# A fused image-and-text kernel on one core: the edge convolution computed from split operands, with its halo rows staged on their own

## The chip, the cores and the metric

The kernel runs on one core of a Trainium2 chip. The metric is the device time of one execution in microseconds. The kernel before takes 2001.3 us, the median of three runs (1999.5 to 2003.4).

## What is computed

Eight images of 256 x 256 pixels and eight texts of 128 tokens go through one small transformer-like chain. The part that the change touches is the first step of each image:

```python
gray = jnp.einsum('bchw,c->bhw', x, w)[:, None]           # w = (0.2989, 0.587, 0.114)
edges = jax.lax.conv_general_dilated(gray, scharr, window_strides=(1, 1), padding='SAME', ...)
edge = jnp.sqrt(jnp.square(edges)).sum(axis=1) / 2        # two 3x3 filters, |.|, added
h = jnp.concatenate([edge, text_embedding], axis=1)       # 256 image rows + 128 text rows = 384 x 256
...                                                       # attention, MLP, ternary FFN, attention, mixture of 8 experts
```

So an image gives 256 rows of 256 numbers, from a gray picture and two 3x3 Scharr filters ("kinds" below: the horizontal and the vertical one). Everything after `h` works on 384 rows per image.

## The kernel before, in words

Every engine has its own program, written out by hand in one order, and engines wait for each other on semaphores. An engine executes in program order, so a wait holds back all that is written behind it on that engine.

**Stages.** A setup (weights, text embeddings, the filter matrices), a prologue for images 0 and 1, then sixteen "units": units 0 to 7 do the first attention and the MLPs, units 8 to 15 the second attention and more. The unit functions interleave three images: in unit u the attention of image u runs beside the MLP of image u-1 and the edge convolution of image u+2. Images 0 and 1 are convolved in setup and prologue, images 2 to 7 in units 0 to 5 (unit 0 is `U_FIRST`, units 1 to 5 are `U_MID0` in a loop). The last third of the time is routing and the expert stage.

**The convolution.** A picture is held as two halves of 128 rows, one row per partition: `gray[128, 2, 258]`, columns with a zero at either side. The sum over the three rows of a filter is a matrix product with a banded 128 x 128 matrix `band[:, k, dx, :]` (kind k, column shift dx). It is a product in full float32. For each half `hf` and kind `k` there are three such products of 256 columns, and a fourth with `edge_w` that brings in the one row of the other half (`halo_gray`, three shifted copies of it on three partitions):

```python
for k in range(2):
    o = ps[bank][:, IMG * k:IMG * (k + 1)]
    for dx in range(3):
        mm(o, band[:, k, dx, :], gray[:, hf, dx:dx + IMG], start=(dx == 0), stop=False)
    last = mm(o, edge_w[:, hf, k, :], halo_gray[:, 1 - hf, :], start=False, stop=True)
```

A PSUM bank (`conv0`, `conv1`) holds one half of the picture, both kinds. ScalarE takes the absolute value of a bank into `edge` (`edges` on ScalarE, line 1640), VectorE adds the two kinds into `h_in` (line 2128).

**Where it stands in a unit.** On VectorE `gray_ahead` (lines 2137 to 2141, three passes over the picture) stands early. SyncE then issues the six halo copies of one row each (`load_halo`, line 642), behind the load of the text rows and ahead of `load_residual` and of the load of the next image. On TensorE the order around it is: `turn(3)`, `attn_rows(2)`, `queries_keys(0)`, `edges(0)`, `scores(3)`, `edges(1)`, `queries_keys(1)`, `queries_keys(2)`, `mix(0)`. `queries_keys(0)` (line 1035, 128x512) needs the normalised, transposed input `xTa`, half of which ScalarE writes in `take_first` (line 1583) and half VectorE (line 2120). On ScalarE the order is `exps(0)`, `take_turned(0)`, `exps(1)`, `exps(2)`, `take_turned(1)`, `exps(3)`, `take_turned(2)`, `take_first`, `exps(4)`, `edge_sizes(0)`, `edge_sizes(1)`, `take_turned(3)`. The banks 6 and 7 of PSUM are handed from one dense product to the next: `conv0` is followed in its bank by `qk_1`, `conv1` by `qk_2`.

**Prologue.** TensorE multiplies `qk_0` to `qk_2` of image 0, then the convolution of image 1, then turns the stacked queries and keys; ScalarE takes the absolute values of image 1 and then writes `stk_q`, `stk_k` (line 1624).

Of the kernel before, what the change touches and what calls it, by code (L numbers as in the profile page):

```python
# [20 lines left out]
F32 = mybir.dt.float32  # L21
# [24 lines left out]
E = 8  # L46
# [22 lines left out]
for _name, _n in (("ident", P), ("rel", S), ("mask", S), ("cos", NT * 2 * HD0), ("sin", NT * 2 * HD0), ("ones", P),  # L69
                  ("shift", 3 * P), ("before", P), ("tiebreak", E * TILES), ("expert_row", E * TILES),  # L70
                  ("scan_keep", 2 * E * TILES), ("count", P), ("token", TILES), ("same_expert", GROUPS), ("bits", SEARCH * STEPS)):
    COLS[_name] = (NC_COLS, NC_COLS + _n)
    NC_COLS += _n
# [4 lines left out]
def shape_constants():  # L78

    c = np.zeros((P, NC_COLS), np.float32)  # L80

    def put(name, value):
        a, b = COLS[name]
        c[:, a:b] = np.asarray(value, np.float32).reshape(P, b - a)

    p = np.arange(P)
    put("ident", np.eye(P))
    rel = (S - P) + p[:, None] - np.arange(S)[None, :]
    put("rel", rel)
# [10 lines left out]
    put("shift", np.stack([np.eye(P, k=1 - dy) for dy in range(3)], 1))  # L100
    put("before", np.triu(np.ones((P, P)), 1))
# [222 lines left out]
FIRST_LOADS = 12  # L324
# [3 lines left out]
def early_fusion_kernel(nc, a, const, out):  # L328
# [23 lines left out]
    with ctx:  # L352
# [14 lines left out]
        def const_cols(name):  # L367
# [30 lines left out]
        (qk, rot2, stk_q, stk_k, img, gray, halo_gray), first_end = region(  # L398
            first_only, ("qk", [P, NT, 512], F32), ("rot2", [P, 512], F32),
            ("stk_q", [P, NT, 8 * 64], F32R), ("stk_k", [P, NT, 8 * 64], F32R),  # L400
            ("img", [P, 3, 2, IMG], F32), ("gray", [P, 2, IMG + 2], F32), ("halo_gray", [3, 2, IMG], F32))
# [5 lines left out]
        assert second_end <= first_end  # L407
        offsets["top"] = first_end
# [7 lines left out]
        band = sb("band", [P, 2, 3, P])  # L416
        edge_w = sb("edge_w", [3, 2, 2, P])
# [6 lines left out]
        edge = sb("edge", [P, 2, 2 * IMG])  # L424
# [25 lines left out]
        (wq1_rot, emb, embT, proj_raw, projT, txt_rows, hashf, hash_i, wq1_raw, rot_tmp, ang, scharr_b, scharr_h, shift_c,  # L450
# [5 lines left out]
            ("ang", [P, 8, H1], F32), ("scharr_b", [P, 2, 3, 3], F32), ("scharr_h", [3, 2, 3], F32),  # L456
            ("shift_c", [P, 3 * P], F32),
# [5 lines left out]
        txt_scale = small[:, 8:9]  # L463
        absum, above, below, gsum = small[:, 0:2], small[:, 2:4], small[:, 4:6], small[:, 6:8]
# [61 lines left out]
        gray_ready = sem("gray_ready")  # L526
        halo_loaded = sem("halo_loaded")
# [103 lines left out]
        def _(sp):  # L631
# [17 lines left out]
            for k, (dst, src) in enumerate((  # L649
# [9 lines left out]
                (scharr_h[:, 0, :], a["L0_tok_scharr"][0, 0].rearrange("a b -> b a")),  # L659
                (scharr_h[:, 1, :], a["L0_tok_scharr"][1, 0].rearrange("a b -> b a")),  # L660
                (shift_c[:], const[:, COLS["shift"][0]:COLS["shift"][1]]),
# [217 lines left out]
        def _(pe):  # L879
# [15 lines left out]
            def convolve(sec, i, img_no, halves):  # L895

                pe.wait_ge(gray_ready, at(img_no, 1, 1))
                pe.wait_ge(halo_loaded, at(img_no, 96, 96))
                for hf in halves:
                    name = f"conv{hf}"  # L900
                    bank = banks.bank(sec, name)
                    banks.wait_free(pe, sec, name, i)
                    for k in range(2):
                        o = ps[bank][:, IMG * k:IMG * (k + 1)]
                        for dx in range(3):
                            mm(o, band[:, k, dx, :], gray[:, hf, dx:dx + IMG], start=(dx == 0), stop=False)  # L906
                        last = mm(o, edge_w[:, hf, k, :], halo_gray[:, 1 - hf, :], start=False, stop=True)  # L907
                    last.then_inc(filled[bank], 1)
# [162 lines left out]
            def unit(sec, i, u, k):  # L1071
# [57 lines left out]
                def edges(hf):  # L1129
                    if k.conv:  # L1130
                        convolve(sec, i, moved(u, 2), (hf,))
# [440 lines left out]
        def _(act):  # L1572
# [61 lines left out]
            def edges(sec, i, img_no, hf):  # L1634


                banks.wait_filled(act, sec, f"conv{hf}", i)
                if img_no[0] is not None or img_no[1] > 0:
                    act.wait_ge(var_ready[LN_FIRST], at(img_no, NT, hf - NT + 1))
                f(edge[:, hf, :], ps[banks.bank(sec, f"conv{hf}")][:], ACT.Abs) \  # L1640
                    .then_inc(freed[banks.bank(sec, f"conv{hf}")], 1)
# [5 lines left out]
            def unit(sec, i, u, k):  # L1647
# [41 lines left out]
                def edge_sizes(hf):  # L1689
                    if k.conv:  # L1690
                        edges(sec, i, moved(u, 2), hf)
# [42 lines left out]
                if k.layer == 0:  # L1734
# [12 lines left out]
                    edge_sizes(0)  # L1747
                    edge_sizes(1)
# [126 lines left out]
            for hf in range(2):  # L1875
                edges(SETUP, 0, (None, 0), hf)
            ln_affine(PRO, 0, "lnA0", xTa[:, 0, :], 0, 2)
            for hf in range(2):
                edges(PRO, 0, (None, 1), hf)
# [70 lines left out]
        def _(dve):  # L1950
# [12 lines left out]
            v.memset(edge_w[:], 0.0)  # L1963
# [99 lines left out]
            shift = shift_c[:].rearrange("p (y m) -> p y m", y=3)  # L2063
            for y_ in range(3):
                for k in range(2):
                    for dx in range(3):
                        w = scharr_b[:, k, y_, dx:dx + 1]
                        if y_ == 0:
                            ts(band[:, k, dx, :], shift[:, 0, :], w, None, ALU.mult)
                        else:  # L2070
                            stt(band[:, k, dx, :], shift[:, y_, :], w, band[:, k, dx, :], ALU.mult, ALU.add)
                then()
            for k in range(2):
                ts(edge_w[:, 0, k, P - 1:P], scharr_h[:, k, 2:3], 0.5, None, ALU.mult)
                ts(edge_w[:, 1, k, 0:1], scharr_h[:, k, 0:1], 0.5, None, ALU.mult)
# [46 lines left out]
            def edges(sec, i, img_no, hf):  # L2122


                banks.wait_taken(dve, sec, f"conv{hf}", i)
                if img_no[0] is not None or img_no[1] > 0:
                    dve.wait_ge(spilled, at(img_no, 32, 0))
                tt(h_in[:, hf, :], edge[:, hf, 0:IMG], edge[:, hf, IMG:2 * IMG], ALU.add)

            def gray_image(c):  # L2130
# [3 lines left out]
                if c[0] is not None or c[1] > 0:  # L2134
                    dve.wait_ge(halo_loaded, at(c, 96, 0))
# [5 lines left out]
                stt(inner, img[:, 2], GRAY[2], inner, ALU.mult, ALU.add).then_inc(gray_ready, 1)  # L2141

# [112 lines left out]
            def unit(sec, i, u, k):  # L2255
# [54 lines left out]

                def edge_sum(hf):
                    if k.conv:
                        edges(sec, i, img_c, hf)
# [112 lines left out]
                if k.layer == 0:  # L2426
# [7 lines left out]
                    second_moments(0)  # L2434
                    take_values(1)
# [18 lines left out]
                    mask_max(6)  # L2454
                    edge_sum(0)
                    mlp_norm(1)
# [7 lines left out]
                    edge_sum(1)  # L2464
# [170 lines left out]
            for hf in range(2):  # L2635
                edges(SETUP, 0, (None, 0), hf)
# [6 lines left out]
            for hf in range(2):  # L2643
                edges(PRO, 0, (None, 1), hf)
# [281 lines left out]
        def _(pool):  # L2926
# [4 lines left out]
            g.memset(gray[:], 0.0)  # L2931
# [247 lines left out]
```

## Time and profile before

| | |
|---|---|
| median of three runs | 2001.3 us (1999.5 to 2003.4) |
| the profiled execution | 1996.8 us, its span 1995.0 us |
| TensorE matmul busy | 1768.5 us (89% of the span) |
| VectorE, ScalarE, GpSimd busy | 62%, 48%, 28% |
| mean granted TensorE clock | 0.943 of full |
| chain that ended last | TensorE 71%, issue 11%, VectorE 8% |

A time in a row is counted from the start of the span. In the timeline, the columns are start, duration, engine, line and operation, out<-in; a number in brackets is the idle time of that engine before it. "xN" are N instructions merged, the duration then being from the first start to the last end. A float32 product shows as two MATMUL records, a product from float32r operands as one. Matmul durations include the way through the array, so the pace of a sequence is read from the starts.

### The profile page before, as it was taken

The page shows a single profiled execution, that of the slowest core. Times are in us where ns is not written, and L with a number is a line of the kernel's source. Part 1 is how long each engine was busy: PE and PEld are TensorE (multiplying, and loading weights), DVE is VectorE, ACT ScalarE, POOL GpSimd, SP SyncE. Part 2 cuts the span into 40 slices and gives each one's busy share as a digit, 9 for nine tenths or more (in the row PEclk, how much of TensorE's full clock was granted, in tenths as well). Part 3 has the DMA queues.
Part 4 walks back from the last instruction along what each step waited for, and adds up shares of the span by engine and source line. Part 5 has one row for each costly group of instructions (what it writes and reads, how often), then busy time and mean ns, then how long its engine had stood idle before and what let it go on. Part 6 is the DMA issues. An engine that isn't in the chain of part 4 may idle for free.

```text
span 1995.0 us, 35526 instructions
## 1 busy us (share of the span) xinstructions
PE 1768.5 (89%) x10970; PEld 1408.1 (71%) x10970; DVE 1237.8 (62%) x4024; ACT 957.3 (48%) x2645; POOL 552.9 (28%) x784
## 2 busy tenths in 40 slices
PE   3457999999999899899999999992499999999997
PEld 2244676767677686667777777771389998999896
DVE  7446686767777676756677776657754454445442
ACT  2025474666657566565666666640033343333331
POOL 2233324242423411211111111001333335434431
PEclk9668999999999999999999999995589999999998
DMA  6100101101010100102100110002212222222210
GB/s 193 56 27 17 51 2 58 35 24 56 3 43 0 56 26 8 33 1 58 33 32 32 32 32 0 24 25 81 73 48 98 81 75 66 77 72 67 61 38 20
DMA packets 74577, 90.44 MB, mean 45 GB/s; under 512 B 16539, under 2 KB 64710, under 8 KB 74472
## 3 DMA queue, kind: packets, MB, share of 16 engines
q1 hardware_dynamic: 65000, 72.49, 11.1%
q0 software_dynamic: 9472, 16.77, 3.0%
q8 instruction: 39, 0.64, 0.1%
q14 instruction: 66, 0.54, 0.1%
HBM read 71.26 MB, written 25.26 MB: 48 GB/s over the span
## 4 chain that ended last, share of the span: by engine, by line
PE 71%; issue 11%; DVE 8%; POOL 3%; ACT 2%; DVEq 2%; DMA 1%; POOLq 1%; SPq 1%; ACTq 0%
PE bank L1035 17%; PE bank L1539 16%; PE bank L1554 9%; PE bank L983 6%; PE bank L967 5%; PE bank L1018 5%; PE bank L1177 2%; PE bank L906 2%; PE bank L994 1%; PE bank L1057 1%; DVE probs L2177 1%; PE bank L891 1%; DVE at_least L2735 1%; PE bank L907 1%; POOL rstd_a L2946 1%
## 5 line engine op out<-in xcount | busy, mean ns | idle before, releaser
L1660 ACT ACTIVATE probs<-probs,nmax 128x128 f32<-128x128 f32 (+2 forms) x768 | 381.0, 501 | 75.3 <-DVE nmax L2177 75.1
L983 PE MATMUL bank<-cst,probs 128*128 128x128 f32 x1536 | 234.5, 279 | 19.4 <-ACT probsT L1668 11.6
L983 PEld LDWEIGHTS bank<-cst,probs 128*128 128x128 f32 x1536 | 182.4, 143 | 68.4 <-issue 25.8
L1539 PE MATMUL bank<-xeT,gate_w 128*128 128x480 f32 x768 | 189.3, 382 | 1.4 <-issue 1.4
L1539 PE MATMUL bank<-xeT,up_w 128*128 128x480 f32 x768 | 188.2, 380 | 0.0
L2272 DVE COPY probsT<-bank 128x384 f32<-128x384 f32 x256 | 141.4, 552 | 74.0 <-PE bank L983 72.4
L1554 PE MATMUL bank<-down_w,hT 128*120 128x256 f32 x1536 | 182.8, 281 | 0.0
L1554 PEld LDWEIGHTS bank<-down_w,hT 128*120 128x120 f32 x1536 | 181.5, 182 | 0.1
L2988 POOL COPY rinv<-rowsum 128x384 f32<-128x384 f32 x80 | 40.7, 509 | 497.3 <-DVE o1T L2199 294.5
L2882 DVE TENSOR_TENSOR prod<-bank,sil 128x480 f32<-128x480 f32 x128 | 83.8, 657 | 150.5 <-PE bank L1539 150.3
L1668 ACT COPY probsT<-bank 128x384 f32<-128x384 f32 x256 | 121.8, 476 | 113.1 <-PE bank L983 104.4
L1539 PEld LDWEIGHTS bank<-xeT,gate_w 128*128 128x128 f32 x768 | 145.4, 190 | 23.2 <-issue 1.8
L1539 PEld LDWEIGHTS bank<-xeT,up_w 128*128 128x128 f32 x768 | 145.8, 190 | 21.9
L1583 ACT ACTIVATE sil<-bank 128x480 f32<-128x480 f32 x128 | 73.1, 571 | 181.5 <-PE bank L1539 181.5
L1660 ACT ACTIVATION_READ_ACCUMULATOR probs<-probs,nmax 128x1 f32 x768 | 147.0, 191 | 0.0
L3148 POOL DMA_INDIRECT out<-ye,slot_token x64 | 77.4, 1210 | 242.8 <-DVE ye L2896 230.9
L2177 DVE CUSTOM_DVE_ANT_0 probs<-bank,alibi 128x128 f32<-128x128 f32 (+2 forms) x384 | 141.2, 420 | 1.8
L2177 DVE CUSTOM_DVE_ANT_0 probs<-bank,cst 128x128 f32<-128x128 f32 (+2 forms) x384 | 140.4, 420 | 0.0
L967 PE MATMUL bank<-k1T,q1T 64*128 64x256 f32 (+2 forms) x768 | 100.5, 394 | 2.7 <-DVE nmax L2177 2.7
L3120 POOL DMA_INDIRECT xe<-xn_rows,slot_token x64 | 71.0, 1109 | 104.5 <-DVEq L2820 68.0
L967 PEld LDWEIGHTS bank<-k1T,q1T 64*128 64x128 f32 x768 | 83.3, 186 | 19.9 <-issue 15.2
L1018 PE MATMUL bank<-probsT,v 128*64 128x384 f32 (+2 forms) x768 | 97.0, 388 | 0.0
(314 smaller groups left out, 3325.1 us busy)
## 6 DMA issues: line engine op xcount, KB each, us to landing
gate_raw<-in_L_ffn_gate_w SPq DMA_DIRECT2D x8, 1024.0 KB, 4.8
up_raw<-in_L_ffn_up_w SPq DMA_DIRECT2D x8, 1024.0 KB, 6.9
down_raw<-in_L_ffn_down_w SPq DMA_DIRECT2D x8, 1024.0 KB, 5.7
img<-in_x SPq DMA_DIRECT2D x8, 768.0 KB, 5.1
residual_rows<-x SPq DMA_DIRECT2D x8, 384.0 KB, 2.5
residual_rows<-h_in SPq DMA_DIRECT2D x8, 384.0 KB, 3.8
xr<-residual_rows SPq DMA_DIRECT2D x8, 384.0 KB, 4.8
hr<-residual_rows SPq DMA_DIRECT2D x8, 384.0 KB, 3.7
```

The lines of the kernel that those rows point to most:

```text
L967: last = mm(scores_place(s, t), q[:, P * t:P * (t + 1)], k[:, 0:P * (t + 1)], start=True, stop=True)
L983: last = tr(ps[bank][:, P * q:P * (q + 1)], probs[:, n % 4, SEG[t] + P * j:SEG[t] + P * (j + 1)], ident)
L1018: last = mm(ps[5][rows_o, P * j:S], w, probsT[:, n % 4, cols_j], start=first, stop=final)
L1035: last = mm(ps[bank][:, 0:width], x, w, start=(k == 0), stop=(k == len(pieces) - 1))
L1539: last = mm(ps[bank][:, 0:HALF], w[:, wp, c, P * m:P * (m + 1)], xeT[:, xp, c, HALF * hf:HALF * (hf + 1)], start=(c == 0 and k == 0), stop ...
L1554: last = mm(ps[bank][:, D * (j % 2):D * (j % 2) + D][0:CP], hT[:, hp, m, CP * j:CP * (j + 1)], down_w[:, wp, m, :], start=(m == 0 and k == ...
L1660: last = f(p, p, ACT.Exp, bias=nmax[:, n % 4, t:t + 1], scale=-1.0, accum_out=rowsum[:, where, t:t + 1])
L1668: nc.scalar.copy(probsT[:, n % 4, 0:3 * P], ps[3][:, 0:3 * P]).then_inc(freed[3], 1)
L2177: last = v.tensor_tensor_reduce(out=probs[:, n % 4, seg(t)], in0=scores_place(n, t), in1=bias[:, P * (2 - t):S], scale=1.0, scalar=BIG, op ...
L2272: v.tensor_copy(probsT[:, n % 4, 3 * P:6 * P], ps[4][:, 0:3 * P]).then_inc(freed[4], 1)
L2882: tt(prod[:, q % 2, :], k[:, 0:HALF], sil[:, q % 2, :], ALU.mult).then_inc(f_, 1)
L3148: g.indirect_dma_start(out_rows, slots(e, j), ye[0:CP, j, :], None, bounds_check=T - 1, oob_is_err=False).then_inc(scattered, 16)
```

## The change

The picture and the filter matrices are split in an upper part in the short format float32r (`gray_hi`, `band[:, 0]`) and the remainder (`gray_lo`, `band[:, 1]`). Three products (hi x hi, hi x lo, lo x hi) take the place of one float32 product, each a single pass, and each over both halves of the picture at once, 512 columns. A bank now holds one kind, both halves. The halo rows of both halves and of all three parts are stacked on 18 partitions (`halo_rows`), spread by ScalarE into the two halves (`halo_halves`), and come in with one product per kind. The upper part of the picture is made on ScalarE (`gray_uppers`), the lower on VectorE (`gray_lowers`). The absolute value of the first kind is written to `h_in`, that of the second stays in its bank, and VectorE adds them from there; that bank is freed by VectorE.

```diff
             def load_halo(i):
-                sp.wait_ge(gray_ready, i + 1)
-                for k, row in enumerate((P - 1, 0)):
-                    for dx in range(3):
-                        sp.dma_start(halo_gray[dx:dx + 1, k, :], gray[row:row + 1, k, dx:dx + IMG]) \
-                            .then_inc(halo_loaded, 16)
+                sp.wait_ge(gray_split, i + 1)
+                if i > 0:
+                    sp.wait_ge(halo_ready, i)
+                for hf, row in enumerate((0, P - 1)):
+                    for part, src in enumerate((gray_hi, gray_lo, gray_hi)):
+                        for dx in range(3):
+                            q = 9 * hf + 3 * part + dx
+                            sp.dma_start(halo_rows[q:q + 1, :],
+                                         src[row:row + 1, 1 - hf, dx:dx + IMG].bitcast(F32)) \
+                                .then_inc(halo_loaded, 16)
...
-                pe.wait_ge(gray_ready, at(img_no, 1, 1))
-                pe.wait_ge(halo_loaded, at(img_no, 96, 96))
...
+                pe.wait_ge(gray_split, at(img_no, 1, 1))
+                pe.wait_ge(halo_ready, at(img_no, 1, 1))
+                for k in kinds:
...
+                    for dx in range(3):
+                        for w, x in ((0, gray_hi), (0, gray_lo), (1, gray_hi)):
+                            mm(ps[bank][:], band[:, w, k, dx, :], x[:, :, dx:dx + IMG],
+                               start=(dx == 0 and w == 0 and x is gray_hi), stop=False)
+                    mm(ps[bank][:], edge_w[:, k, :], halo[:], start=False, stop=True).then_inc(filled[bank], 1)
...
+            def halo_halves(img_no):
+                act.wait_ge(halo_loaded, at(img_no, 16 * HALO_LOADS, 16 * HALO_LOADS))
+                for hf in range(2):
+                    last = f(halo[:, hf, :], halo_rows[:], ACT.Identity, bias=0.0, scale=halo_side[:, hf:hf + 1])
+                last.then_inc(halo_ready, 1)
+
+            def gray_uppers(img_no):
+                act.wait_ge(gray_ready, at(img_no, 1, 1))
+                nc.scalar.copy(gray_hi[:, :, 1:IMG + 1], gray[:, :, 1:IMG + 1]).then_inc(gray_upper, 1)
...
                     exps(1)
+                    gray_upper_part()
                     exps(2)
                     take_turned(1)
                     exps(3)
                     take_turned(2)
+                    halo_parts()
                     take_second()
                     take_first()
                     exps(4)
                     take_queries(0)
-                    edge_sizes(0)
-                    edge_sizes(1)
+                    edge_sizes()
...
+            def gray_lowers(c):
+                dve.wait_ge(gray_upper, at(c, 1, 1))
+                inner = slice(1, IMG + 1)
+                tt(gray_lo[:, :, inner], gray[:, :, inner], gray_hi[:, :, inner].bitcast(F32), ALU.subtract).then_inc(gray_split, 1)
...
                     take_turned(0)
                     second_moments(0)
+                    gray_lower_part()
                     take_values(1)
...
                     mask_max(6)
+                    mlp_norm(1)
                     edge_sum(0)
-                    mlp_norm(1)
+                    edge_sum(1)
                     first_moments(0)
...
             for t in range(NT):
                 queries_keys_of(PRO, 0, t)
-            for hf in range(2):
-                edges(PRO, 0, (None, 1), hf)
+            gray_lowers((None, 1))
+            edges(PRO, 0, (None, 1))
```

In setup the filter matrices are split too (on VectorE: a copy and a subtraction of 768 columns and some ten tiny instructions, where four tiny ones stood), and there are four more small loads ahead of `first_loaded`. `gray` now lies where `gray_lo` lies.

## Rows read from the trace of the kernel before

**Rows 1.** The page's second part: busy tenths of TensorE and its granted clock, 40 slices.

```profile
PE   3457999999999899899999999992499999999997
...
PEclk9668999999999999999999999995589999999998
```

**Rows 2.** Busy time by stretch, one unit: length, busy us of each engine, clock, DMA.

```profile
483.40:571.90 88.50, 84.61 (x540) 63.38 (x540) 64.75 (x225) 54.94 (x160) 30.78 (x51) 1.00 0.11 33
```

**Rows 3.** Timeline of TensorE in unit 5, around the convolution of image 7.

```profile
585.33 1.88 PE L1035 MATMUL bank<-wqkv,xTa 128*128 128x512 f32 x4
587.05 1.46 PE L906 MATMUL bank<-gray,band 128*128 128x256 f32 x6
...
591.18 0.82 PE L967 MATMUL bank<-k0T,q0T 64*128 64x256 f32 x6
591.93 1.56 PE L906 MATMUL bank<-gray,band 128*128 128x256 f32 x6
...
596.16 3.70 PE L1035 MATMUL bank<-wqkv,xTa 128*128 128x512 f32 x8
```

**Rows 4.** Timeline of the expert stage on TensorE: six products of 480 columns, twice.

```profile
1474.62 1.46 PE L1539 MATMUL bank<-xeT,up_w 128*128 128x480 f32 x6
1475.92 1.46 PE L1539 MATMUL bank<-xeT,gate_w 128*128 128x480 f32 x6
```

**Rows 5.** Timelines of VectorE and ScalarE in unit 5, before the convolution.

```profile
578.16 0.69 DVE L2141 SCALAR_TENSOR_TENSOR gray<-img,gray 128x512 f32<-128x512 f32 x1
...
582.17 0.48 ACT L1668 COPY probsT<-bank 128x384 f32<-128x384 f32 x1 [0.35 <-PE bank L983]
583.64 0.67 ACT L1583 ACTIVATE xTa<-bank,cols 128x384 f32<-128x384 f32 x1 [0.99 <-PE bank L891]
```

**Rows 6.** The halo copies: timeline in unit 5, duration of all 48, time to landing.

```profile
578.88 3.66 SPq L642 DMA_DIRECT2D halo_gray<-gray  x6
...
L642 SPq DMA_DIRECT2D halo_gray<-gray x48: 497/589/1174, 59.1 to 582.0; - x48
...
DMA to landing us min/median/max: 1.6/1.7/2.4
```

**Rows 7.** Groups by form: busy us, mean ns of one, idle before.

```profile
L1581 ACT CAST f1T<-bank 128x512 fp32r<-128x512 f32 x4 | 2.3, 586 | 3.5 <-PE bank L942 3.5
...
L1624 ACT CAST stk_k<-qk 128x256 fp32r<-128x256 f32 x48 | 16.2, 403 | 0.0
...
L2887 DVE TENSOR_TENSOR hT<-prod,hT 128x480 fp32r<-128x480 f32 x128 | 83.2, 650 | 2.5 <-ACT hT L1929 2.0
...
L2377 DVE CAST hid_parts<-relu 128x384 fp32r<-128x384 f32 x32 | 11.4, 358 | 8.8 <-ACT relu L1583 8.7
```

**Rows 8.** Granted clock by stretch (length, TensorE busy, clock), and one timeline row.

```profile
71.00:72.00 1.00, 1.00 (x3) 0.60 0.00 0
...
146.00:147.00 1.00, 1.00 (x7) 0.56 0.32 86
...
141.56 1.19 PE L967 MATMUL bank<-k0T,q0T 64*128 64x256 f32 x6 [8.71 <-DVE nmax L2177]
```

**Rows 9.** Timeline of unit 0, image 2: end of the gray picture, first query-key product.

```profile
146.66 0.69 DVE L2141 SCALAR_TENSOR_TENSOR gray<-img,gray 128x512 f32<-128x512 f32 x1
...
151.91 1.94 PE L1035 MATMUL bank<-wqkv,xTa 128*128 128x512 f32 x4
```

**Rows 10.** Timeline of setup and prologue, images 0 and 1.

```profile
58.41 0.69 DVE L2141 SCALAR_TENSOR_TENSOR gray<-img,gray 128x512 f32<-128x512 f32 x1
...
64.30 2.90 PE L906 MATMUL bank<-gray,band 128*128 128x256 f32 x6 [15.19 <-DMA halo_gray<-gray]
...
76.41 0.60 ACT L1640 ACTIVATE edge<-bank 128x512 f32<-128x512 f32 x1 [3.56 <-PE bank L907]
...
99.00 0.69 DVE L2203 TENSOR_TENSOR qk<-bank,rows 128x512 f32<-128x512 f32 x1 [1.02 <-PE bank L1035]
...
111.02 1.01 ACT L1624 CAST stk_q<-qk 128x256 fp32r<-128x256 f32 x3 [3.16 <-POOL qk L2979]
```

More of the change, by code:

```diff
@@ L100, in shape_constants @@
     put("shift", np.stack([np.eye(P, k=1 - dy) for dy in range(3)], 1))
+    halo = np.zeros((P, 3))
+    for k in range(2):
+        halo[9 * k:9 * k + 9, k] = 1.0
+        halo[9 * k + 6:9 * k + 9, 2] = -1.0
+    put("halo", halo)
     put("before", np.triu(np.ones((P, P)), 1))
@@ L397, in early_fusion_kernel @@
         first_only = offsets["top"]
-        (qk, rot2, stk_q, stk_k, img, gray, halo_gray), first_end = region(
+        (qk, rot2, stk_q, stk_k, img, gray_hi, gray_lo, halo_rows, halo), first_end = region(
             first_only, ("qk", [P, NT, 512], F32), ("rot2", [P, 512], F32),
             ("stk_q", [P, NT, 8 * 64], F32R), ("stk_k", [P, NT, 8 * 64], F32R),
-            ("img", [P, 3, 2, IMG], F32), ("gray", [P, 2, IMG + 2], F32), ("halo_gray", [3, 2, IMG], F32))
+            ("img", [P, 3, 2, IMG], F32), ("gray_hi", [P, 2, IMG + 2], F32R), ("gray_lo", [P, 2, IMG + 2], F32R), ("halo_rows", [18, IMG], F32),
+            ("halo", [18, 2, IMG], F32R))
         (k1T, v1, _, q1T, x_moe, wq1, wk1, wv1), second_end = region(
@@ L407, in early_fusion_kernel @@
         assert second_end <= first_end
+        (gray,), _ = region(first_end - 4 * 3 * IMG - 32 * 65, ("gray", [P, 2, IMG + 2], F32))
         offsets["top"] = first_end
@@ L463, in early_fusion_kernel @@
         txt_scale = small[:, 8:9]
+        halo_side = small[0:18, 32:34]
         absum, above, below, gsum = small[:, 0:2], small[:, 2:4], small[:, 4:6], small[:, 6:8]
@@ L526, in early_fusion_kernel @@
         gray_ready = sem("gray_ready")
+        gray_upper = sem("gray_upper")
+        gray_split = sem("gray_split")
+        halo_ready = sem("halo_ready")
+        edge_ready = sem("edge_ready")
         halo_loaded = sem("halo_loaded")
@@ L893, in transposed, with convolve @@
                             last.then_inc(filled[bank], 1)
-            def convolve(sec, i, img_no, halves):
-                pe.wait_ge(gray_ready, at(img_no, 1, 1))
-                pe.wait_ge(halo_loaded, at(img_no, 96, 96))
-                for hf in halves:
-                    name = f"conv{hf}"
+            def convolve(sec, i, img_no, kinds):
+                pe.wait_ge(gray_split, at(img_no, 1, 1))
+                pe.wait_ge(halo_ready, at(img_no, 1, 1))
+                for k in kinds:
+                    name = f"conv{k}"
                     bank = banks.bank(sec, name)
                     banks.wait_free(pe, sec, name, i)
[L903 to L908, printed above, removed]
+                    for dx in range(3):
[3 more added lines that the diff above has]
+                    mm(ps[bank][:], edge_w[:, k, :], halo[:], start=False, stop=True).then_inc(filled[bank], 1)
             pe.wait_ge(first_loaded, 16 * FIRST_LOADS)
@@ L1127, in stack, with edges @@
                         stack_turned(sec, i, img_b, hh, t, x)
-                def edges(hf):
+                def edges(kind):
                     if k.conv:
-                        convolve(sec, i, moved(u, 2), (hf,))
+                        convolve(sec, i, moved(u, 2), (kind,))
                 def attn_rows(t):
@@ L1687, in take_stack, with gray_upper_part, halo_parts, edge_sizes @@
                         take_stack_of(sec, i, hh, t)
-                def edge_sizes(hf):
+                def gray_upper_part():
                     if k.conv:
-                        edges(sec, i, moved(u, 2), hf)
+                        gray_uppers(moved(u, 2))
+                def halo_parts():
+                    if k.conv:
+                        halo_halves(moved(u, 2))
+                def edge_sizes():
+                    if k.conv:
+                        edges(sec, i, moved(u, 2))
                 def take_mlp():
@@ L1873, in unit @@
                     relu_of(7)
-            for hf in range(2):
-                edges(SETUP, 0, (None, 0), hf)
+            gray_uppers((None, 0))
+            halo_halves((None, 0))
+            edges(SETUP, 0, (None, 0))
             ln_affine(PRO, 0, "lnA0", xTa[:, 0, :], 0, 2)
-            for hf in range(2):
-                edges(PRO, 0, (None, 1), hf)
+            gray_uppers((None, 1))
+            halo_halves((None, 1))
+            edges(PRO, 0, (None, 1))
             for hh in range(2):
@@ L1962, in _ @@
             v.memset(tok[:, :, 0:1], 0)
-            v.memset(edge_w[:], 0.0)
+            v.memset(small[:, 34:36], 0.0)
+            v.memset(edge_f[:], 0.0)
             v.memset(eps[:], EPS)
@@ L2120, in ln_affine, with edges @@
                     ts(dst, k[:, 0:S], cols[:, g:g + 1], cols[:, b:b + 1], ALU.mult, ALU.add).then_inc(f_, 1)
[L2122 to L2128, printed above, removed]
+            def edges(sec, i, img_no, halves=range(2)):
+                dve.wait_ge(edge_ready, at(img_no, 1, 1))
+                k, f_ = bank_of(sec, "conv1", i)
+                for hf in halves:
+                    last = tt(h_in[:, hf, :], h_in[:, hf, :], k[:, IMG * hf:IMG * (hf + 1)], ALU.add)
+                if 1 in halves:
+                    last.then_inc(f_, 1)
             def gray_image(c):
@@ L2309, in gray_ahead, with gray_lower_part @@
                         gray_image(img_c)
+                def gray_lower_part():
+                    if k.conv:
+                        gray_lowers(img_c)
                 def edge_sum(hf):
                     if k.conv:
-                        edges(sec, i, img_c, hf)
+                        edges(sec, i, img_c, (hf,))
                 def first_moments(t):
@@ L2634, in _ @@
             gray_image((None, 0))
-            for hf in range(2):
-                edges(SETUP, 0, (None, 0), hf)
+            gray_lowers((None, 0))
+            edges(SETUP, 0, (None, 0))
             embed((None, 0))
@@ L2642, in _ @@
                 queries_keys_of(PRO, 0, t)
-            for hf in range(2):
-                edges(PRO, 0, (None, 1), hf)
+            gray_lowers((None, 1))
+            edges(PRO, 0, (None, 1))
             for hh in range(2):
```

67 lines of the change are left out of this document (42 added, 25 removed).

## The prediction, made before the change was run

> **What bounds the kernel now.** I read the page's second part first. The reader sees TensorE at nine tenths or more from slice 5 to slice 26, which holds all units but the first two, at a granted clock of nine tenths or more; setup and prologue are the slices before, where TensorE is half idle and the clock is lower [rows 1]. Then the busy times of one unit: TensorE works 84.6 us of 88.5, and no other engine gets above 65 [rows 2]. So in units 0 to 5, where images 2 to 7 are convolved, TensorE sets the pace, and what its program waits for anywhere is added to the end. Last I read the timelines around the convolution, engine by engine, since the change puts new steps into the programs of all of them [rows 3, 5, 6].
>
> **What TensorE gains.** `edges(0)` runs from 587.05 to 591.18 and `edges(1)` from 591.93 to 596.16: 4.13 + 4.23 = 8.4 us per image [rows 3]. The new products are of the kind of the expert stage: six of 480 columns from one start to the next take 1.30 us, 0.217 each [rows 4], so 512 columns take 0.217 x 512/480 = 0.231 us. Two kinds of 9 + 1 products are 20 x 0.231 = 4.6 us. The gain is 3.7 us per image at full clock.
>
> **What now stands before the convolution.** The new chain, in unit 5: VectorE ends the gray picture at 578.16 + 0.69 = 578.85 [rows 5]. (1) `gray_uppers` on ScalarE, a cast of 512 columns, 0.59 [rows 7]; with the handover 0.65. It stands behind `exps(1)`, which is over by then. (2) `gray_lowers` on VectorE: 0.65 us for 480 columns [rows 7], so 0.7, with the handover 0.75. (3) SyncE may only now issue the copies, and there are 18 instead of 6. Six take 3.66 us from first start to last end, one takes 0.59 [rows 6]: the starts are (3.66 - 0.59)/5 = 0.61 apart. 17 such steps are 10.4 us; the first issue of a row is one of the short ones (497 ns the shortest), so the later steps are a little longer than the mean, and I take 10.7. (4) The last copy lands 1.7 us after its issue [rows 6]. (5) `halo_halves` on ScalarE, two instructions of 256 columns; the nearest is the cast of 256 columns, 0.40 each [rows 7]: 0.8. In all 0.65 + 0.75 + 0.05 + 10.7 + 1.7 + 0.8 = 14.65 us, so `halo_ready` comes at 593.5 in the old count of time.
>
> **Who waits for it.** The convolution itself would have been reached at 587.05. But `halo_halves` stands on ScalarE between `take_turned(2)`, which ends at 582.65, and `take_first`, which ran at 583.64 [rows 5]. So ScalarE stands still for about ten us, and behind it in its program are `take_first`, `exps(4)` and the absolute values. `take_first` (0.67) writes `xTa`, for which TensorE's `queries_keys(0)` waits, one step ahead of the convolution. That product starts at 593.5 + 0.7 = 594.2 instead of 585.33 [rows 3]: TensorE is held 8.9 us. VectorE runs dry too, because it waits for TensorE's products, so nobody has work in hand that could shorten the unit afterwards.
>
> **The clock after the hold.** TensorE has then been idle for some 8 us. In unit 0 it was idle 8.71 us before 141.56, and the clock, at half, is back at full only within the slice from 146 to 147, of which 0.56 on average means a change at 146.9 less a little, say 146.4 to 146.9 [rows 8]: five us at 1.2 instead of 2.4 GHz, 2.4 us lost. After the 15.19 us of idleness in setup it is back within the slice from 71 to 72, seven us after 64.30, 3.6 us lost [rows 8, 10]. The low bound is no loss at all. I take 2.4, the nearest row by length of idleness.
>
> **Per unit.** 8.9 + 2.4 - 3.7 = +7.6 us for images 3 to 7 (the distance from the gray picture to `queries_keys(0)`, 6.5 us in unit 5, repeats in the four other units of the loop within half a microsecond), 5 x 7.6 = 38. For image 2 the distance is 151.91 - 147.35 = 4.6 us instead of 6.5 [rows 9], so the hold is 10.8 and the sum +9.5. Units together: +47.5.
>
> **Setup, image 0.** VectorE's program is solid here. A cast of 768 columns is twice 0.36 and a subtraction of 768 about 1.0, from the forms of 384 and 480 columns [rows 7]; with some ten tiny instructions in place of four, 2.6 in all (2 to 3.5). From the end of the gray picture (59.10) TensorE started after 5.2 us [rows 10]; now after 14.65 + 0.4 for slightly slower issues here = 15.1: +9.9. The convolution took 64.3 to 76.4, mostly at half clock; 20 products, seven us of them at half clock (0.462 each), are 8.3 us: -3.8. Both sums on VectorE now follow the second absolute value, where one did: +0.4. The four extra small loads ahead of `first_loaded` would be 4 x 0.6 = 2.4 if all their issue counted; the big loads ahead of them fill the time, and I take 0.3. Together +9.4.
>
> **Prologue, image 1.** `gray_lowers` stands behind the third `queries_keys` of VectorE, which ends at 99.7 [rows 10]. From there 0.7 + 0.05 + 10.7 + 1.7 + 0.8: the convolution starts at 113.7, after 14 us without work, so again at half clock for most of its way, 7.1 to 8.3 us, and ends at 121 to 122. Two absolute values later, at 122.3, ScalarE begins `stk_q`, which ran at 111.02 [rows 10]: +11.3. Full clock would make it +8.
>
> **What I cost at nothing.** The bank of `conv1` is freed by VectorE after two sums, not by ScalarE: about 0.7 + 0.85 after the last product, while `qk_1` runs 1.7 us ahead of `qk_2`, its next user; without that cover it is a few tenths per unit. VectorE's wait for `gray_upper` and its subtraction delay `take_values(1)` by 0.9 us; the hold covers it, without a hold it would be 0.9 per unit. ScalarE is 0.6 us later in `exps(2)`; the same holds. `load_residual` and the next image sit on SyncE's queue behind 12 more copies, 7.5 us later; the first is wanted only with the MLP rows and so falls back less than TensorE, the second a unit later. The sum +47.5 + 9.4 + 11.3 = +68.2 is made on the profiled execution, 1996.8 us (span 1995.0 and 1.8 around it), and gives 2065; the median of the runs lies 4.5 us above that execution, so I predict **2069 us**.
>
> **A rule against this.** The profile shows SyncE occupied for 0.59 us by every one-row copy [rows 6]. The Trainium skill (DMA: Bandwidth & Descriptors, "Anatomy of one DMA", written for the gpsimd path) says that dispatch is small, about 50 ns, that many descriptors can be sent before it shows, and that nearly all of the fixed two microseconds is the wait for the write to be confirmed. By that rule 18 copies would land hardly later than one, and the hold would vanish; it is the first rival below. The row shows the time of the issue itself on this queue, and I go by the row.
>
> **Rivals.**
> (a) *The issues overlap and the chain hides.* Then `halo_ready` comes 0.65 + 0.75 + 1.7 + 0.8 + a little = 4 us after the picture, before the 6.5 us are over. Units: -3.7 + 0.9 each, six times, -17; setup 2.6 + 0.3 - 1 - 3.8 + 0.4 = -1.5; prologue nothing. Time 1983. For it speaks only that the data are 1 KB each; against it the six back-to-back issues. The point from which it decides is the sum of the issues: hold and gain cancel at 5.5 us for 17 steps, 0.32 us apart, half of what is seen. 4%.
> (b) *Held, but milder.* The clock does not fall, or recovers sooner (-2.4 x 6, -3 in the prologue), or issues come 0.50 apart, the shortest of 48 [rows 6] (17 x 0.13 x 8 = -18). One of them gives about 2050, both 2035. 20%.
> (c) *Held harder.* Some issues take up to 1.17 us [rows 6]; a mean of 0.73 adds 17 x 0.1 x 8 = 14; seven us of low clock add 1.2 x 6 = 7. Time 2076 to 2090. 17%.
> (d) *The products don't run at the pace of the expert stage.* At twice 0.231 us the convolution costs 9.2 us, +4.6 x 8 = +37, 2106. Against it speaks a row of the same form [rows 4]. 4%.
> (e) *A partly hidden hold, to within 0.2%* (4 us, about what can be told from no change): 2%.
> My forecast, within 10 us of 2069, has 53%.
>
> **Range.** From (b)'s double case to above (c): 2037 to 2092, with a little over 8 in 10. Faster by over 0.2%: (a), 4%; within 0.2%: (e), 2%; slower: 94%.
>
> **What would show it.** In a unit: 18 halo issues over 11 us; ScalarE idle about ten us before two 18x256 instructions; TensorE idle eight us before `queries_keys(0)` and the clock at half for the next five; the convolution itself 4.6 us where the clock is full; idle time ahead of the first expert unchanged. Most likely to make me wrong: another pace of 18 issues, which counts eight times.

## The result, and the profile after

| | kernel before | changed kernel |
|---|---|---|
| median of the runs | 2002.3 us (1999.5 to 2005.1) | 2095.3 us (2093.5 to 2099.6) |
| profiled execution, its span | 1996.8 us, 1995.0 us | 2095.4 us, 2093.6 us |
| mean clock granted to TensorE | 0.943 | 0.918 |

The ratio is 1.0467, 95% interval 1.0445 to 1.0490: the change made the kernel 4.7% slower. The forecast was slower, 2069 us with 2037 to 2092 as the range; the sign is right, the median lies 3 us above the range. From profile to profile the loss is 98.6 us, where the sum said 68.2.

The page's second part after the change, 40 slices, stands beside [rows 1]:

```profile
PE   3255779879797999989999999996269999999997
...
PEclk9557699999999999999999999998569999999998
```

The stretch of low clock at the start is one slice longer and a step lower, and in the units up to slice 13 TensorE shows more digits of seven and eight. Busy time of one unit (columns as in [rows 2]):

```profile
455.20:553.80 98.60, 85.92 (x534) 64.17 (x532) 65.47 (x227) 56.51 (x163) 30.59 (x51) 0.93 0.10 30
```

A unit takes 98.6 us instead of 88.5, and TensorE is busy in it for 1.3 us more only, at a mean clock of 0.93. So about nine us are idleness. Where they lie, the timelines of unit 5 show. First TensorE, from the last work before the hold (the stretch in which TensorE waits) to the end of the convolution; in brackets the idle time before, and what ended it:

```profile
656.85 1.13 PE L1053 MATMUL bank<-wo,o0T 128*128 128x256 f32 x4 [0.61 <-DVE vpad L2296]
...
660.39 0.76 PE L910 MATMUL bank<-cst,xh_a 128*128 128x128 f32 x5 [0.79 <-DVE vpad L2296]
661.00 0.82 PE L1001 MATMUL bank<-cst,probs 128*128 128x128 f32 x6
670.41 2.08 PE L1053 MATMUL bank<-wo,o0T 128*128 128x256 f32 x4 [8.59 <-ACT xTa L1601]
672.27 3.62 PE L1053 MATMUL bank<-wqkv,xTa 128*128 128x512 f32 x4
674.91 1.42 PE L924 MATMUL bank<-gray_hi,band 128*128 128x512 f32 x1
...
679.40 0.50 PE L924 MATMUL bank<-gray_hi,band 128*128 128x512 f32 x1
...
681.71 0.50 PE L926 MATMUL bank<-halo,edge_w 18*128 18x512 f32 x1
682.13 3.70 PE L1053 MATMUL bank<-wqkv,xTa 128*128 128x512 f32 x8
```

ScalarE and SyncE in the same stretch:

```profile
655.05 0.62 ACT L1660 CAST gray_hi<-gray 128x512 fp32r<-128x512 f32 x1 [0.39 <-DVE gray L2200]
...
668.89 0.91 ACT L1655 ACTIVATE halo<-halo_rows,small 18x256 fp32r<-18x256 f32 x2 [9.20 <-DMA halo_rows<-gray_hi]
669.71 0.65 ACT L1601 ACTIVATE xTa<-bank,cols 128x384 f32<-128x384 f32 x1
```

```profile
656.42 1.77 SPq L660 DMA_DIRECT2D halo_rows<-gray_hi  x3
...
665.87 1.85 SPq L660 DMA_DIRECT2D halo_rows<-gray_hi  x3
```

The reader sees the chain as it was forecast: picture, cast, subtraction, 18 issues from 656.42 to 667.72, landing, and two instructions of ScalarE that stood 9.20 us before a wait, with `take_first` behind them. But the first product behind the hold is not `queries_keys(0)`: it is one of `wo` and `o0T`, `attn_rows(2)`.

Second, a stretch with which the change has nothing to do. Waits in layer 1 (VectorE runs its units 9 to 14 as a loop) and the route to the experts: of TensorE, then of VectorE; the numbers are us in all, times, longest:

```profile
PE bank L985 <- DVE nmax L2241: 5.5, 5, 1.3
PE bank L1012 <- POOL rinv L3056: 4.6, 5, 1.0
```

```profile
DVE rowsum L2255 <- issue: 9.6, 5, 2.0
...
DVE probs L2241 <- issue: 2.7, 5, 0.7
```

None of these four stands there in the kernel before, although the instructions of that loop are the same, in the same order. "Issue" is time in which an engine waited for nothing that the profile shows. The page counts 92 packets on the instruction queue instead of 66, and 25 of them fall between 1067 and 1340 us, where there were 2 in the same stretch (980 to 1253) before.

### The profile page after: what moved, and what is told of

Read it like the earlier page. It is cut to its first block, busy times and chain, and to the rows that moved or that the text cites. A ratio compares the mean times of both kernels' runs of the same rounds, so it can differ in the third digit from the quotient of the medians.

```text
span 2093.6 us, 35492 instructions
## 1 busy us (share of the span) xinstructions
PE 1773.8 (85%) x10874; PEld 1408.4 (67%) x10874; DVE 1245.2 (59%) x4040; ACT 969.5 (46%) x2669; POOL 551.5 (26%) x783
## 3 DMA queue, kind: packets, MB, share of 16 engines
q1 hardware_dynamic: 68102, 72.59, 10.8%
## 4 chain that ended last, share of the span: by engine, by line
PE 61%; issue 12%; DVE 8%; POOL 6%; SPq 4%; POOLq 2%; ACT 2%; DMA 2%; DVEq 1%; ACTq 0%
PE bank L1557 16%; PE bank L1053 14%; PE bank L1572 9%; PE bank L1001 5%; PE bank L1036 5%; PE bank L985 5%; SPq L660 3%; PE bank L1195 2%; POOL rot L3039 1%; PE bank L1075 1%; DVE probs L2241 1%; PE bank L1012 1%; DVE at_least L2804 1%; POOL qk L3047 1%; POOL rstd_a L3014 1%
## 5 line engine op out<-in xcount | busy, mean ns | idle before, releaser
L1053 PE MATMUL bank<-wqkv,xTa 128*128 128x512 f32 (+1 forms) x192 | 87.8, 596 | 15.9 <-ACT xTa L1601 10.4
```

What stands on the lines that cost most here:

```text
L1053: last = mm(ps[bank][:, 0:width], x, w, start=(k == 0), stop=(k == len(pieces) - 1))
```

## The experiments

Each ratio is to the kernel before.

**Two first tries on the layer-1 loop.** The edit, ahead of VectorE's loop over units 9 to 14, with 13 in the kernel before and 64 in the changed one:

```diff
+            for _ in range(13):
+                v.nop()
             with dve.Fori(0, MID1) as i:
```

> The kernel before with 13 empty instructions put into VectorE's program just ahead of its loop of layer-1 units (13 is by how much the change lengthened that program). Theory (code loading): the loop of units 9 to 14 no longer stays loaded, VectorE stands still 2.0 us at each of 5 jumps back, TensorE waits about 1 us for rinv and 1 us for nmax after each; +10 to +12 us, about 2013. Rival: the loss in layer 1 comes from the changed memory places or from the late start of layer 1, not from the length of the program; then 13 empty instructions cost nothing, 2002.

> The changed kernel with 64 empty instructions at the same place, so that the loop lies in other blocks of the program again. Theory (code loading): the waits for rinv and nmax in units 9 to 14 go, -10 to -12, the 64 instructions cost at most 3 once: 2084 to 2088. Rival (memory places or lateness): 2095 or a little above.

Measured: 1998.8 us, 0.9993 (0.9977 to 1.0010), and 2095.0 us, 1.0469 (1.0442 to 1.0497). Nothing follows from this about the loop: the empty instructions are not in the built programs (the second profile counts 35492 instructions, as that of the changed kernel does), so both runs repeat the old programs, and show how well the times hold. The same two experiments with one-element memsets, which are kept, 17 in the kernel before and 64 in the changed one:

```diff
+            for j in range(17):
+                v.memset(small[32 * (j // 32):32 * (j // 32) + 1, 36 + j % 32:37 + j % 32], 0.0)
             with dve.Fori(0, MID1) as i:
```

> The kernel before with 17 one-element memsets of an unused place in VectorE's program just ahead of its loop of layer-1 units; with them the loop lies exactly where it lies in the changed kernel (the changed kernel's program for VectorE is 17 instructions longer up to there; the empty instructions of the first try were dropped when the program was built, so that it was the kernel before). Theory (code loading by the place of the loop): VectorE stands still some 2 us at each of 5 jumps back, TensorE waits for rinv and nmax after each, +10 to +12: 2012 to 2014. Rival (memory places or lateness): 1 us for the memsets at most, 2001 to 2003.

> The changed kernel with 64 such memsets at the same place (a first try with empty instructions left the program as it was), so that the loop begins at the start of a block of 256 instructions. Theory (code loading): the stands of VectorE and the waits of TensorE for rinv and nmax in units 9 to 14 go, -10 to -12, the memsets cost 1 to 3 once: 2084 to 2087. Rival: 2095 to 2098.

Measured: 2011.3 us, 1.0053 (1.0035 to 1.0071), which is 10.3 us more than before; and 2083.5 us, 1.0405 (1.0384 to 1.0425), 11.7 us less than the changed kernel. Waits of VectorE and TensorE in the kernel before with 17 memsets, over the layer-1 stretch:

```profile
DVE rowsum L2191 <- issue: 9.7, 5, 2.0
```

```profile
PE bank L967 <- DVE nmax L2177: 7.1, 6, 1.5
PE bank L994 <- POOL rinv L2990: 4.7, 5, 1.0
```

The waits appear with the 17 memsets and go with the 64. The instruction queue has 91 packets instead of 66 in the first, 68 instead of 92 in the second. So 10 to 12 us of the loss come from where the loop of layer 1 lies in VectorE's program, which by my count the change made 17 instructions longer ahead of it (13 by the first count). The Trainium skill (Runtime: NRT & Kernel Launch, "Instruction fetch mechanics") says that instructions are fetched in blocks of 256, that two blocks are held, and that a jump to a block not held must wait for it. The trace agrees as to the kind of wait: five stands of some 2 us, 62 us apart, one for each jump back of a loop of six. Which places of the loop are free of the waits the runs do not show, beyond the three tried: the old one, 17 instructions on, and 64 beyond that.

Waits of the same look stand in the kernel before as well, in the loop of units 1 to 5, one for each of its four jumps back. VectorE and, behind it, TensorE:

```profile
DVE rowsum L2193 <- issue: 12.3, 4, 3.3
```

```profile
PE bank L994 <- POOL rinv L2988: 11.5, 4, 3.1
```

They are in every version here, and no run tried to remove them. That another place of this loop would free up to 11 us is an estimate from these rows, not shown. They matter below, because the clock sometimes falls behind them.

**The wait on ScalarE moved behind `take_queries(0)`.**

```diff
                     take_turned(2)
-                    halo_parts()
                     take_second()
                     take_first()
                     exps(4)
                     take_queries(0)
+                    halo_parts()
                     edge_sizes()
```

> The changed kernel, but ScalarE's wait for the halo rows and its two copies stand directly ahead of the absolute values, behind take_first, exps(4) and take_queries(0). Theory (the hold is one of program order on ScalarE): the chain from the gray picture to halo_ready stays at 14.7 us, but TensorE now does attn_rows(2) and queries_keys(0), about 3 to 4 us of work, before it stops at the convolution; -3.5 in each of five units, -2 in unit 0: about 2075 (2071 to 2080). Rival 1: the clock falls as long, and VectorE or ScalarE run dry anyway, so nothing is gained: 2095. Rival 2: the hold is not set by this chain at all: 2095.

Measured: 2080.4 us, 1.0396 (1.0372 to 1.0421), 15 us less than the changed kernel. TensorE in unit 5:

```profile
648.29 1.88 PE L1053 MATMUL bank<-wqkv,xTa 128*128 128x512 f32 x4
655.68 0.79 PE L924 MATMUL bank<-gray_hi,band 128*128 128x512 f32 x1 [5.52 <-ACT halo L1655]
```

The products that were held are now done first, and the idle time is 5.5 instead of 8.6 us. From unit 2 on the gray pictures follow one another at 95.2 to 95.6 us instead of 98.5 to 98.9: there the order on ScalarE is worth 3.3 us a unit, close to the 3.5 expected. In unit 1 it is worth 0.7 only, because the clock stayed at half for longer behind the hold. The chain is there still.

**Six copies of three rows.**

```diff
-                        for dx in range(3):
-                            q = 9 * hf + 3 * part + dx
-                            sp.dma_start(halo_rows[q:q + 1, :],
-                                         src[row:row + 1, 1 - hf, dx:dx + IMG].bitcast(F32)) \
-                                .then_inc(halo_loaded, 16)
+                        q = 9 * hf + 3 * part
+                        rows = src[row:row + 1, 1 - hf, 0:IMG].bitcast(F32)
+                        rows = bass.AP(rows.tensor, rows.offset, [list(rows.ap[0]), [1, 3], [1, IMG]])
+                        sp.dma_start(halo_rows[q:q + 3, :], rows).then_inc(halo_loaded, 16)
```

> The changed kernel, but with 6 halo copies of three shifted rows each instead of 18 of one row; the same bytes, the order on ScalarE as in the changed kernel. Theory (SyncE pays 0.6 us per copy, whatever it holds): 12 copies less make the chain 7.5 us shorter, 7.2 instead of 14.7 us; the hold in a unit falls from 9.9 to 2.4 and the clock does not fall, so a unit takes 88.6 + 2.4 - 2.9 = 88.1; setup loses 2 instead of 9.4, the prologue 5.6 to 7 instead of 14; with the 12 us of layer 1 that stay, about 2016 (2012 to 2024). Rival: the time goes by row, a copy of three rows takes 1.8 us; then all stays as it is, 2095.

Measured: 2030.0 us, 1.0143 (1.0116 to 1.0170): 65 us of the 93 are gone. The halo copies (ns shortest/median/longest), then TensorE in unit 5:

```profile
L661 SPq DMA_DIRECT2D halo_rows<-gray_hi x32: 630/631/842, 64.2 to 601.5; - x32
```

```profile
604.76 2.08 PE L1052 MATMUL bank<-wo,o0T 128*128 128x256 f32 x4 [1.28 <-ACT xTa L1600]
606.63 2.66 PE L1052 MATMUL bank<-wqkv,xTa 128*128 128x512 f32 x4
```

A copy of three rows occupies SyncE for 0.63 us, one of a single row for 0.59 [rows 6]: the price is by the copy. The hold is 1.28 us. But the time is 14 us above what I expected. In this unit `attn_rows(2)` takes 2.08 us where its like takes 1.13 at full clock: the granted clock is 0.50 from 605 to 608 and 0.91 in the next microsecond. The four units before it do not show that. Their holds were 0.72 to 1.30 us, and behind each of them the same four products ran at full clock. In three of these units the clock had fallen earlier, behind TensorE's stand for `rinv`. Unit 4 has both:

```profile
502.28 0.85 PE L1011 MATMUL bank<-cst,rinv 128*128 128x128 f32 x3 [2.77 <-POOL rinv L3055]
502.92 1.91 PE L1052 MATMUL bank<-wqkv,xTa 128*128 128x256 f32 x4
...
515.48 1.13 PE L1052 MATMUL bank<-wo,o0T 128*128 128x256 f32 x4 [1.28 <-ACT xTa L1600]
```

So neither stand brings the clock down by itself each time. Added up over slices of a microsecond (TensorE's busy time times the missing share of the clock), 10.7 us are lost to it between 230 and 700 us, against 1.5 in the same stretch of the kernel before (215 to 680). These 9 us are the largest piece of what the expectation lacked; the waits for `vpad` (0.6 to 0.8 us, once or twice a unit) and unit 0 (4.7 us longer than before) are others. Why the clock falls behind one such stand and not behind the next stays open.

**Both together.**

> Six copies of three rows and ScalarE's wait directly ahead of the absolute values, both together; VectorE's program as in the changed kernel. Theory: halo_ready comes 7.3 us after the gray picture, TensorE reaches the convolution 8.2 us or more after it, so nothing is held; what stays of the cost in a unit are the two waits for vpad behind gray_lowers, 1.4 us, against a convolution 2.9 us shorter: a unit takes 87.1, 2.5 to 3 less than with six copies alone, 2012 to 2016 in all. Rival: the 1.4 us of waits are enough to bring the clock down for 4 us, 2 us a unit: 2024 to 2028.

Measured: 2046.2 us, 1.0230 (1.0209 to 1.0251), 16 us more than with six copies alone. Both theories missed. ScalarE in unit 5:

```profile
614.94 0.67 ACT L1600 ACTIVATE xTa<-bank,cols 128x384 f32<-128x384 f32 x1 [1.40 <-PE bank L909]
619.27 0.40 ACT L1690 ACTIVATE probs<-probs,nmax 128x128 f32<-128x128 f32 x1 [3.67 <-DVE nmax L2240]
...
620.76 0.89 ACT L1654 ACTIVATE halo<-halo_rows,small 18x256 fp32r<-18x256 f32 x2
```

`halo_parts` has no wait of its own any more, but it stands behind `exps(4)`, which waits for a maximum of VectorE. TensorE stood 3.38 us before the convolution, and then the clock was low from 621.9 to 631. In units 1 to 4 the same stand of 3.37 to 3.40 us was followed by about three us at half clock in three cases and by none at all in the fourth (530 us). One microsecond each (length, TensorE busy, TensorE weight load, VectorE, ScalarE, GpSimd, clock, DMA share, GB/s):

```profile
622.00:623.00 1.00, 1.00 (x3) 0.81 (x4) 0.00 (x0) 0.00 (x0) 1.00 (x2) 0.50 0.00 0
...
630.00:631.00 1.00, 1.00 (x3) 0.75 (x3) 0.00 (x0) 0.00 (x0) 0.00 (x0) 0.51 0.00 0
631.00:632.00 1.00, 1.00 (x4) 0.37 (x2) 0.00 (x0) 0.00 (x0) 0.00 (x0) 1.00 0.00 0
```

**The same with the other losses taken away.** The last kernel, with `gray_lowers` behind the first `queries_keys` of the prologue and behind `take_values(1)` in a unit, and with the 64 memsets:

```diff
             for t in range(NT):
                 queries_keys_of(PRO, 0, t)
-            gray_lowers((None, 1))
+                if t == 0:
+                    gray_lowers((None, 1))
...
-                    gray_lower_part()
                     take_values(1)
+                    gray_lower_part()
```

> As the last, and besides: gray_lowers behind take_values(1) in a unit, in the prologue gray_lowers behind the first of the three queries_keys of VectorE, and 64 memsets ahead of the layer-1 loop. Theory: no wait for vpad (-1.4 x 6), no code loading in layer 1 (-10), the prologue's convolution is no longer behind the queries_keys (-4 to -8): 1983 to 1995, that is 0.3 to 0.9% faster than the kernel before. Rival (the clock or another wait takes the place of those removed): 2005 or more.

Measured: 2035.5 us, 1.0158 (1.0135 to 1.0180). The prologue and layer 1 gave what they were to give (`stk_q` began at 112.95 instead of 120.07, and the layer-1 waits are gone), but the hold of 3.38 us was the same, and the last units took 95.5 us: the clock now stayed at half for nine us behind it in four units, and over units 1 to 5 it took back nine us of what was gained (26.8 lost, counted as above, against 18.0). Four edits at once told less here than the next three did.

**The two instructions between `take_first` and `exps(4)`.** Six copies, and:

```diff
-                    halo_parts()
                     take_second()
                     take_first()
+                    halo_parts()
                     exps(4)
```

> Six copies of three rows, and ScalarE's two halo instructions directly behind take_first, ahead of exps(4). Theory: behind exps(4) they stood behind the maxima of VectorE (ScalarE waited 3.67 us for nmax and came to them 12 us after the gray picture, the rows having landed at 6.5); ahead of exps(4) they run 7.5 us after the picture, 1.5 to 2 us before TensorE reaches the convolution. No hold, clock at full: a unit 88.6 - 2.9 + 1.4 (the waits for vpad behind gray_lowers) = 87.1; 2012 to 2017. Rival: the 1.4 us of waits bring the clock down by themselves; 2022 to 2030.

> As the last, with the 64 memsets ahead of the layer-1 loop and gray_lowers behind the first queries_keys of the prologue. Theory: -11 (code) and -7 (prologue, as in the run before): 1994 to 1999, faster than the kernel before by 0.1 to 0.4%. Rival with the clock: 2004 to 2012.

> As the last, and in a unit gray_lowers behind take_values(1). Theory: one of the two waits for vpad (0.6) goes, the halo comes 0.9 us later and stays just hidden: -0.6 x 6 against the last, 1990 to 1996. Rival: halo_halves now comes later than TensorE, a short hold, and with it the clock: above the last by 5 or more.

Measured: the first, 2017.9 us, 1.0088 (1.0070 to 1.0105); the second, with memsets and prologue, 1998.4 us, 0.9988 (0.9977 to 0.9999); the third, with `gray_lowers` behind `take_values(1)` too, 2001.2 us, 1.0003 (0.9992 to 1.0014). The second is the best version. Its gain of 0.12% is too small to count (its executions lie between 1995 and 2001 us, those of the kernel before between 1996 and 2005), but it is the changed convolution at no loss. The third has no hold either; it lost 7.7 us to the clock over these units where the second lost 4.6, which is about its distance from it. TensorE and ScalarE in unit 5 of the second:

```profile
583.70 0.77 PE L909 MATMUL bank<-cst,xh_a 128*128 128x128 f32 x5 [0.78 <-DVE vpad L2295]
...
586.08 1.88 PE L1052 MATMUL bank<-wqkv,xTa 128*128 128x512 f32 x4
587.40 0.80 PE L923 MATMUL bank<-gray_hi,band 128*128 128x512 f32 x1
```

```profile
584.39 0.67 ACT L1600 ACTIVATE xTa<-bank,cols 128x384 f32<-128x384 f32 x1 [1.40 <-PE bank L909]
584.96 0.89 ACT L1654 ACTIVATE halo<-halo_rows,small 18x256 fp32r<-18x256 f32 x2
```

`halo_ready` comes at 585.85, 1.5 us before TensorE wants it, and no wait for `halo` is left in a unit. Even so a unit takes 88.0 to 89.0 us (88.5 to 89.7 before), not the 87.1 that I expected: 0.8 to 1.4 us go to the waits for `vpad` behind `gray_lowers` (0.2 to 0.4 before), and in unit 5 the clock is 0.77 from 570 to 575 and 0.88 from 575 to 580, behind the same stand for `rinv` (2.79 us) that left it at 1.00 in the kernel before (2.81 us). Nearly all of the gain of the products is used up.

## Why the prediction was right in kind and too low in size

**The chain: right.** Forecast 14.65 us from the end of the gray picture to `halo_ready`; in unit 5 it is 655.02 to 669.80, 14.8. That it costs by the number of copies is shown by the six-copy run, and the first rival, by which the issues overlap and the time would be 1983, has fallen. The Trainium skill (DMA: Bandwidth & Descriptors, "Anatomy of one DMA") gives some 50 ns for the dispatch of a DMA on the gpsimd path. That figure can't be carried over to SyncE's queue: here each copy occupies the engine for 0.59 to 0.63 us. The point from which I said that rival decides, 5.5 us of issues, held only with the place on ScalarE mended: at 4.0 us of issues a unit still lost 0.5 to 1.7 us in the one place, and in the other it lay between 1.1 us gained and 0.4 lost.

**Per unit: +10.1 where +7.6 was forecast.** Image 3's unit to image 7's (units 1 to 5), with 0.3 us in the units behind them, lost 50.5 us instead of 38. In unit 5 three terms give it:

- The hold, 8.9 forecast. I said that the first work to wait would be `queries_keys(0)`. It is `attn_rows(2)`, which writes the bank that `take_first` has to empty; the program gave me the bank, and I followed only the data. It began at 584.36 in the kernel before and at 670.41 here; the picture came 76.17 later, so the hold is 670.41 - 584.36 - 76.17 = 9.9.
- The clock, 2.4 forecast. It is 0.50 from 670.4 to 676 and 0.80 in the next microsecond, so half clock until 676.4 at the most: 5.8 to 6 us, 2.9 lost. In the other four units it was 4.9 to 5.8 us.
- The gain, 3.7 forecast. `conv1` at full clock takes 679.40 to 682.13, 2.73 us for ten products, not 2.31. Most follow at 0.235 us; the first and the one beside the 18-row product are 0.33 to 0.34 apart. With 5.5 us per image the gain is 2.9.

9.9 + 2.9 - 2.9 = 9.9, against a measured 9.5 to 10.3 per unit, from gray picture to gray picture. The close agreement is partly luck: the clock also fell behind the stand for `rinv` in two of these units (355 to 359 and 454 to 458, 1.7 us lost each), which is in none of the three terms, and in the kernel before in one (1.5 us).

**Unit 0: +12.8, forecast +9.5.** `queries_keys(0)` came 15.8 us after the picture instead of 4.6, a hold of 11.2 where I had 10.8. And the clock fell a second time, at 250: 0.50 over 250 to 255, where the same work before ran at 1.00. That was in no term. The best version has such a fall too (218 to 222), without any hold ahead of it, and the run with six copies and the late wait has none there; so a long hold is not needed for it, and its cause stays open.

**Setup: right in sum, by luck to the tenth.** The first `BATCH_NORM_STATS2` came at 86.88 instead of 77.53, +9.35 against +9.4. The chain itself was right (15.1 us from the picture to the first product, as forecast), but two misses cancel: the picture ended 3.6 us later where I had 2.9, and the convolution gave 4.5 us back where I had 3.8.

**Prologue: +14.1, forecast +11.3.** All 20 products ran at half clock, 124.36 to 134.0 or 9.7 us, where 8.3 was the most that I allowed; `gray_lowers` took 1.05 instead of 0.7, and the third `queries_keys` came 0.7 later than setup explains. That its place behind `queries_keys` was the cost is borne out by the runs that moved it: with six copies `stk_q` began at 120.1 to 123.0, and with the move too at 112.7 to 115.6, against 111.02 before.

**What was in no term: layer 1, +11.8.** This is the step that failed. My sum ended with unit 5, and I took code that the change does not touch to cost nothing. From 995.6 us of the changed kernel on, 11.8 us were added, and the two runs with memsets show 10 to 12 for the place of the loop alone. Without it the changed kernel takes 2083.5 us, inside the range, though still 14 above the 2069 of the forecast: the mis-sized terms above are the rest.

In all 2.8 (setup and prologue) + 3.3 + 12.5 + 11.8 = 30.4, the distance from 68.2 to 98.6.

## What to carry to other kernels

Count the copies of a chain, not their bytes: three shifted rows in one copy cost what one row costs, and 12 copies fewer took away two thirds of this loss. When an engine is to wait, look at what stands behind the wait in its program and at who waits for each bank or buffer that it would free, not only for its data; and put the waiting instruction where its input has just arrived, since both a place too early and one too late cost time (2030 and 2046 us against 2018). A loop that nobody touched can become slower because code ahead of it grew: look at "issue" waits and the instruction queue's packets before explaining a loss by the change itself.

## What the runs showed of the hardware that was not expected

- The length of one stand of TensorE does not tell how long the clock stays low behind it. Behind stands of 8.1 to 9.1 us it was at half for 4.9 to 6.0 us. Behind five stands of 3.4 us in one run it was at half for about three us three times, for nine once, and not at all once. Behind five of 0.7 to 1.3 us in another it fell once, for 3.4 us, which cost 1.6.
- Two stands of the same length, ahead of the same work, can differ: of the four stands of 2.8 to 3.1 us for `rinv`, the clock fell behind one in the kernel before, behind two in the changed one, behind three with six copies and behind two in the best version.
- Seventeen one-element memsets ahead of a loop of six units cost 10.3 us, by five waits of 2 us at its jumps back, with 25 more packets on the instruction queue.
- A halo copy of 1 KB and one of 3 KB take 0.59 and 0.63 us of SyncE.
